# Block inversion of 8 triangular 128x128 matrices: full tiles against 64x64 quadrants

## The reference

```
x = silu(causal_conv(hidden @ w_qkvz));  q, k, v, z = split(x)
beta = sigmoid(b);  g = -exp(A_log) * softplus(a + dt_bias)
for t in positions:                       # per value head
    state = state * exp(g_t)
    delta = (v_t - state.T k_t) * beta_t
    state = state + outer(k_t, delta)
    o_t   = state.T q_t
y = rmsnorm(o * silu(z)) @ w_out
```

## Time and profile before

| what | value |
|---|---|
| three runs | 3936.69 us median, 3885.03 to 3954.14 |
| span of the profiled execution | 3551.5 us, the only time that its page gives |
| busy: PE, PE loads, DVE, ACT, POOL | 3065.3, 2458.8, 3248.5, 1811.4, 1861.5 us |
| mean granted clock of TensorE | 0.935 of full speed |
| DMA | 435.09 MB, mean 123 GB/s |

### The profile page before, as it was taken

One profiled execution on the slowest core, in us unless ns is written; L12 is line 12 of the kernel. 1 busy time (PEld: TensorE's weight loads), 2 busy tenths in 40 slices (PEclk: granted clock), 3 DMA queues, 4 the chain that ended last, 5 costly groups with the idle time before them and its releaser, 6 DMA issues.

```text
span 3551.5 us, 58967 instructions
## 1 busy us (share of the span) xinstructions
PE 3065.3 (86%) x18512; PEld 2458.8 (69%) x18512; DVE 3248.5 (91%) x10343; ACT 1811.4 (51%) x4134; POOL 1861.5 (52%) x1973
## 2 busy tenths in 40 slices
PE   6761799989998899989999898989999899989997
PEld 3330577767777677767777777777777677777776
DVE  7888899989999899989999899989998899989997
ACT  2231455545555455555555555555555555555554
POOL 0001565556665566545665555655556555565555
PEclk8885799999999999999999999999999999999999
DMA  1000555545554455444554454445454454544554
GB/s 58 1 1 25 135 139 137 136 121 147 133 136 129 123 144 133 129 121 134 147 133 132 132 135 133 131 119 141 131 143 127 125 141 130 143 127 137 135 141 136
DMA packets 550338, 435.09 MB, mean 123 GB/s; under 512 B 250976, under 2 KB 457824, under 8 KB 549984
## 3 DMA queue, kind: packets, MB, share of 16 engines
q1 hardware_dynamic: 483424, 226.34, 23.9%
q0 software_dynamic: 66560, 204.54, 20.9%
HBM read 350.93 MB, written 45.74 MB: 112 GB/s over the span
## 4 chain that ended last, share of the span: by engine, by line
DVE 58%; PE 27%; issue 8%; POOL 3%; DMA 3%; DVEq 1%; SPq 1%; ACT 0%; POOLq 0%; ACTq 0%
DVE qkv L1082 12%; PE ps L523 6%; DVE rows L1098 6%; PE ps L510 6%; PE ps L530 6%; DVE mix L1110 5%; DVE outer L1119 5%; DVE xr L1123 5%; PE ps L476 4%; DVE xg L1052 3%; DVE E L1070 2%; DVE acc L1047 2%; POOL rows L857 2%; PE ps L493 2%; DVE acc L1183 2%
## 5 line engine op out<-in xcount | busy, mean ns | idle before, releaser
L857 POOL DMA_INDIRECT rows<-table,pick x1040 | 1047.2, 1007 | 363.9 <-issue 335.7
L715 ACT ACTIVATE qkv<-qkv 128x512 f32<-128x512 f32 x260 | 163.8, 630 | 710.8 <-DVE qkv L1082 710.8
L1082 DVE SCALAR_TENSOR_TENSOR qkv<-raw,cwv,qkv 128x510 f32<-128x510 f32 (+2 forms) x390 | 467.5, 1199 | 6.9
L530 PE MATMUL ps<-XT,E 128*128 128x128 f32 x3072 | 412.2, 282 | 0.0
L510 PEld LDWEIGHTS ps<-X,AT 128*128 128x128 f32 x3072 | 375.4, 197 | 51.0 <-issue 42.3
L523 PEld LDWEIGHTS ps<-E,XT 128*128 128x128 f32 x2048 | 270.0, 202 | 165.1 <-DVE E L1070 132.4
L530 PEld LDWEIGHTS ps<-XT,E 128*128 128x128 f32 x3072 | 381.5, 198 | 0.0
L510 PE MATMUL ps<-X,AT 128*128 128x128 f32 x3072 | 381.2, 278 | 0.3 <-DMA XT<-whole 0.3
L1110 DVE SCALAR_TENSOR_TENSOR mix<-rows,zc,mix 128x256 f32<-128x256 f32 x896 | 374.9, 475 | 0.0
L523 PE MATMUL ps<-E,XT 128*128 128x128 f32 x2048 | 293.2, 289 | 83.6 <-DVE E L1070 83.6
L710 ACT ACTIVATE raw<-ps 128x512 f32<-128x512 f32 x260 | 155.2, 597 | 342.8 <-PE ps L476 342.4
(11 more groups left out here) (167 smaller groups left out, 6844.2 us busy)
## 6 DMA issues: line engine op xcount, KB each, us to landing
Wvz<-wvz SPq DMA_DIRECT2D x65, 512.0 KB, 3.2
xb<-xnT SPq DMA_DIRECT2D x65, 512.0 KB, 4.3
whole<-AT SPq DMA_DIRECT2D x130, 256.0 KB
X<-whole SPq DMA_DIRECT2D x130, 256.0 KB, 3.3
XT<-whole SPq DMA_DIRECT2D x130, 256.0 KB, 4.0
Wkq<-wkq SPq DMA_DIRECT2D x66, 256.0 KB, 3.6
rows<-table,pick POOLq DMA_INDIRECT x1040
wo<-woh SPq DMA_DIRECT2D x65, 256.0 KB, 4.0
```

The source lines that it names most:

```text
L530: done = mm(ps[:, 4 + g, (a % 4) * P:(a % 4 + 1) * P], E[:, a, :], src[:, a, :], start=True, stop=True)
L857: pool.indirect_dma_start(rows[:, m, :], None, table[:, :], bass.IndirectOffsetOnAxis(ap=pick[:, m:m + 1], axis=0)).then_inc(gathered, 16)
L1082: ins = V.scalar_tensor_tensor(out=o, in0=i, scalar=w, in1=o, op0=ALU.mult, op1=ALU.add)
```

## The change

The levels of 16 and 32 are done on the two diagonal 64x64 quadrants alone, with a tile of 64 columns for each of 8 tasks, so that a result for all tasks fits one bank. A matmul takes rows 0 to 63 or 64 to 127 of its operands and writes the same partitions. Of E only the columns of the first block of each pair come out of matmuls (32 of 64, `firsts`); the others are the identity, copied once into E16 and E32 at the start. The last level becomes one 64x64 corner: minus (A's corner times X64 of the lower half) is copied by ACT with scale -1, and XT of the upper half times it gives the corner of XT. XT's other corner is set to zero once. The lower quadrant alone is needed in X64. Y gets a buffer of its own. X16 and XT16 are read as quadrants, by four DMAs as before, of half the bytes. Waits follow: PE now waits for ACT's `e_s` where it waited for DVE's fifth `e_v`, and the wait on `acc_v` for bank 3 and that on `qs_s` stand later on PE; POOL waits for the whole of level 32 (`e_v` 2).

```
+    H = P // 2;  lower, upper = slice(0, H), slice(H, P);  halves = (lower, upper)
+        def firsts(ap, n):
+            return ap.rearrange("p a (b s c) -> p a b s c", s=2, c=n)[:, :, :, 0, :]
-                    sp.wait_ge(sm["xt_t"], at("xt_t", 2))
-                for g in range(2):
-                    for s, dst in enumerate((X16, XT16)):
-                        sp.dma_start(dst[:, 4 * g:4 * g + 4, :], matrices(1 + s, g)).then_inc(sm["inv_in"], 16)
+                    sp.wait_ge(sm["xt_t"], at("xt_t", 1))
+                for s, dst in enumerate((X16, XT16)):
+                    for h in halves:
+                        sp.dma_start(dst[h, :, :], matrices(1 + s)[h, :, h]).then_inc(sm["inv_in"], 16)
...
                 def level_E(lv):
-                    src = X16 if lv == 0 else X
-                    for g in range(2):
-                        if lv:
-                            pe.wait_ge(sm["x_s"], at("x_s", 2 * (lv - 1) + g + 1))
-                        for a in range(4 * g, 4 * g + 4):
-                            done = mm(ps[:, g, (a % 4) * P:(a % 4 + 1) * P], AT_b[:, a, :], src[:, a, :], start=True, stop=True)
-                        done.then_inc(sm["e_t"], 1)
+                    src, n = ((X16, 16), (X32, 32))[lv]
+                    if lv:
+                        pe.wait_ge(sm["x_s"], at("x_s", lv))
+                    for a in range(TASKS):
+                        for h in halves:
+                            done = mm(ps[h, 0, a * 32:a * 32 + 32], AT_b[h, a, h], firsts(src[h, a:a + 1, :], n),
+                                      start=True, stop=True)
+                    done.then_inc(sm["e_t"], 1)
...
+                def level_X(lv):
+                    src, E = ((XT16, E16), (XT32, E32))[lv]
+                    if lv:
+                        pe.wait_ge(sm["xt_s"], at("xt_s", lv))
+                    pe.wait_ge(sm["e_v"], at("e_v", lv + 1))
...
+                    for a in range(TASKS):
+                        for h in halves[:2 - lv]:
+                            done = mm(ps[h, 2, a * H:(a + 1) * H], src[h, a, :], E[h, a, :], start=True, stop=True)
+                    done.then_inc(sm["x_t"], 1)
...
+                    for a in range(TASKS):
+                        for h in halves:
+                            done = mm(ps[h, 4, a * H:(a + 1) * H], E[h, a, :], src[h, a, :], start=True, stop=True)
+                    done.then_inc(sm["xt_t"], 1)
+                def corner_E():
+                    pe.wait_ge(sm["x_s"], at("x_s", 2))
+                    for a in range(TASKS):
+                        done = mm(ps[upper, 0, a * H:(a + 1) * H], AT_b[lower, a, upper], X64[lower, a, :], start=True, stop=True)
+                    done.then_inc(sm["e_t"], 1)
+                def corner_XT():
+                    pe.wait_ge(sm["xt_s"], at("xt_s", 3))
+                    pe.wait_ge(sm["e_s"], at("e_s", 1))
+                    for a in range(TASKS):
+                        done = mm(ps[lower, 4, a * H:(a + 1) * H], E64[upper, a, :], XT[upper, a, upper], start=True, stop=True)
                     done.then_inc(sm["xt_t"], 1)
...
-                    level_X(1, 0)
-                    level_X(1, 1)
-                    level_E(2)
+                    level_X(1)
+                    corner_E()
+                    if place["u"]:
+                        pe.wait_ge(sm["acc_v"], last("acc_v", 2))
...
-                    pe.wait_ge(sm["e_v"], at("e_v", 5))
+                    pe.wait_ge(sm["e_s"], at("e_s", 1))
...
+                def compact(dst, bank, h=slice(0, P), scale=1.0):
+                    return A(dst, ps[h, bank, :].rearrange("p (a i) -> p a i", a=TASKS), ACT.Copy, scale=scale)
+                def take_X(lv):
+                    act.wait_ge(sm["x_t"], at("x_t", lv + 1))
+                    if lv == 0:
+                        compact(X32[:, :, :], 2).then_inc(sm["x_s"], 1)
+                    else:
+                        compact(X64[lower, :, :], 2, lower).then_inc(sm["x_s"], 1)
+                def take_XT(lv):
...
+                    elif lv == 1:
+                        for h in halves:
+                            compact(XT[h, :, h], 4, h).then_inc(sm["xt_s"], 1)
+                    else:
+                        compact(XT[lower, :, upper], 4, lower).then_inc(sm["xt_s"], 1)
+                def take_corner():
+                    act.wait_ge(sm["e_t"], at("e_t", 3))
+                    compact(E64[upper, :, :], 0, upper, -1.0).then_inc(sm["e_s"], 1)
...
-                def level(lv, g):
-                    dve.wait_ge(sm["e_t"], at("e_t", 2 * lv + g + 1))
-                    V.tensor_tensor(E[:, 4 * g:4 * g + 4, :], ps[:, g, :].rearrange("p (a i) -> p a i", a=4), mask(C_MS + lv, 4), ALU.mult)\
-                        .then_inc(sm["e_v"], 1)
+                def level(lv):
+                    E, n = ((E16, 16), (E32, 32))[lv]
+                    dve.wait_ge(sm["e_t"], at("e_t", lv + 1))
+                    m = cst[:, T_MS + 32 * lv:T_MS + 32 * lv + 32].rearrange("p (b c) -> p b c", c=n)
+                    V.tensor_tensor(firsts(E[:, :, :], n), ps[:, 0, 0:256].rearrange("p (a b c) -> p a b c", a=TASKS, c=n),
+                                    m.unsqueeze(1).broadcast_to([P, TASKS, 32 // n, n]), ALU.mult).then_inc(sm["e_v"], 1)
...
-                    level(2, 0)
-                    level(2, 1)
                     expert_mix(4, 6)
```

More of the change, by code:

```diff
@@ L69, in level @@
     def level(n):
-        off = (p // (2 * n) == j // (2 * n)) & (p // n == j // n + 1)
-        return np.eye(P) - off
+        q, c = p % H, np.array([c for c in range(H) if c // n % 2 == 0])[None, :]
+        off = (q // (2 * n) == c // (2 * n)) & (q // n == c // n + 1)
+        return (q == c) - 1.0 * off
     eye = np.broadcast_to(np.eye(BL).reshape(1, BL * BL), (P, BL * BL))
-    m = [np.eye(P), p <= j, p > j, p < j, eye[:, :P], eye[:, P:]] + [level(n) for n in LEVELS]
+    m = [np.eye(P), p <= j, p > j, p < j, eye[:, :P], eye[:, P:]]
     m = np.stack([np.asarray(a, np.float32) for a in m], 1).reshape(P, NC * P)
@@ L361, in _ @@
             clear(GROUPS)
[L362 to L364 removed]
+            sp.wait_ge(zeroed, 1)
+            for s in range(2):
+                sp.dma_start(matrices(1 + s), XT[:, :, :]).then_inc(loaded, 16)
             sp.wait_ge(loaded, LOADS + 32)
@@ L611, in one_pass @@
                     pe.wait_ge(sm["S_s"], at("S_s", 1))
+                    if place["u"]:
+                        pe.wait_ge(sm["qs_s"], last("qs_s"))
                     for w, bank in ((KCH, 1), (QCH, 5)):
@@ L757, in one_pass @@
                 if back:
-                    for g in range(2):
-                        take_X(1, g)
-                        take_XT(1, g)
+                    take_X(1)
+                    take_XT(1)
+                    take_corner()
                 silu(1)
```

101 lines of the change are left out of this document (43 added, 58 removed).

## The result

The changed kernel took 4173.36 us in the median of 4 runs (4170.59 to 4181.92), the kernel before 3944.86 in 4 runs on the same chip (3885.03 to 3954.14): a ratio of 1.0645, with a 95% interval of 1.0597 to 1.0694. It is slower by 229 us, where I forecast 38 less.

A forecast was written before the change was run, and what follows sets the result against it. Neither PE nor DVE alone was taken to bound the kernel; the chain alternates between them. Earlier steps summed to 0.6 us a pass, 64 x 0.6 = 38 us off 3936.69, about 3900 us; range 3785 to 4000.

The forecast's parts named there:

- what lies around the span (385 us): Runs' median lies 385 us above the profiled span of 3551.5; taken as outside it and unchanged by the edit.
- the corner's new wait: Last level: PE waits for ACT's copy of the corner product; costed at nothing, 0.6 us without cover.
- The record's price: PE's 64-column records: 0.056 us each, between 0.028 and 0.111; 208 cost 11.6 us a pass, for 14.2 before.
- Rival 1: PE's levels: two quadrants run side by side, 0.04 us or less a record; some 100 us gained, 3840; chance 0.29.
- the mask on the first products: DVE's mask after the levels of 16 and 32: claimed to come only 0.27 us earlier in a pass.
- the 200 us forecast: DVE's level operations: six of 0.66 us become two of 0.41, removing 3.1 us a pass, 200 us in all.
- DVE's busy time falling by less than some 200 us: Sign that the forecast is wrong: DVE's busy time over the run doesn't fall by some 200 us.
- the two acc sums: DVE's sums into acc beside POOL's xg products: first slips out short, second is held long.
- Borders between tile sizes: PE entering or leaving small tiles, eight a pass: 0.2 us each, between 0 and 0.27, covered by gaps or slack.
- The elimination: DVE's elimination after the acc sums: claimed to get going about 0.5 to 0.7 us earlier in a pass.
- Rival 2: PE between first E and products: records don't halve; gain gone at 62 ns, 4350 us at 0.111; chance 0.15.
- Rival 3: PE's granted clock falls to 1.2 GHz in the level stretches: 100 to 200 us lost, 4040 to 4140; chance 0.06.

The follow-up runs named there:

- e5: Changed kernel, no edit, run on chip 14: 3515.89 us, 0.9818 of the kernel before.
- e10: Changed kernel, no edit, run on chip 0: 3510.08 us, 0.9803 of the kernel before.
- e17: Changed kernel with the transposed X of the level of 32 computed three times, 64 more records a pass, on chip 11: 4043.43 us in one run.
- E64: Not a run: the last level's corner product, minus A's corner times X of the lower half, copied by ACT with scale -1; no time of its own.
- e16: Changed kernel without the gathers of expert rows, on chip 11: 3392.4 us in one run.
- e3: Changed kernel without the gathers of expert rows, on chip 13: 3405.91 us, 0.9493 of the kernel before.
- e15: Changed kernel with the lower quadrant for all tasks first, then the upper, in both levels, on chip 11: 4137.22 us in two runs.
- e18: Changed kernel with two pairs of expert mixes moved ahead of the masks on the products, on chip 11: 4159.9 us, 1.0705 of the kernel before.
- e12: Changed kernel with two pairs of expert mixes moved ahead of the masks on the products, on chip 0: 3483.5 us, 0.9733 of the kernel before.
- e2: Changed kernel with the lower quadrant for all tasks first, then the upper, in both levels, on chip 13: 3733.21 us, 1.0406 of the kernel before.
- e8: Changed kernel with 24 unread filler matmuls a pass added where PE waits: 3592.53 us, 1.0045 of the kernel before.

## Why the prediction was wrong

**The step that failed** is "I take what lies around the span (385 us) as unchanged". The prediction moved a sum made on one chip to a median from another. The profiled execution of before is one of a chip on which this kernel takes 3580; the timed runs came from one on which it takes 3945. On chips of the first sort (e5, e10) the change gives 0.98 of before, the direction that the working gave: 63 and 66 us, where it said 38. On the second sort 4 us a pass are lost. What I took as unchanged, the distance between the two kinds of chip, is 366 us in the kernel before (3944.86 - 3579.04) and 657 in the changed one (4173.36 - 3515.89): it grew by 291.7 us, and that less the gain of 63.2 is the measured loss of 228.5. One sign was there to read: a span far below the lowest timed run (3885) says that the two may not be the same population. The result brought the other: every run has about 2 us around its span, none anything near 385. The very execution whose trace I summed is among e5's runs of before, 3553.28 us on chip 14; e5's profiled run is 37 us shorter. That this meets the forecast 38 is luck: the records, the borders, the first mask and the sums into acc each came out otherwise, as told below, and 3553.28 is among the fastest of 19 runs whose median is 3579.04.

**What the slow kind adds.** Passes, as the mean distance of two zc (L1133, L1179): before 49.07 us in the first profile, 54.74 on chip 11; the changed kernel 48.57 on chip 14, 58.89 in its first profile. So the chip costs before 5.7 us a pass and the changed kernel 10.3. (54.74 and 58.89 are from two chips that agree on before within 1%, 3912 and 3945; no run timed both kernels on chip 11.) Where it comes in, as medians over 63 passes, each time from the pass's zc (fast is the first profile):

```
                                 before, fast / chip 11     changed, chip 14 / first chip
mask on the first products          10.1 / 10.7                8.5 /  9.5
mask on the second products, kq     20.4 / 25.7               18.6 / 26.1
gated outputs                       30.8 / 35.9               29.6 / 42.2
expert dots of the next pass        43.9 / 49.5               42.7 / 54.2
```

Up to kq before loses 4.7 us beyond what it lost at the first mask, the changed kernel 6.5; from there to the gated outputs (L1052, L1096) before loses nothing more, the changed kernel another 5.1. The late increments come 11.4 to 11.9 us in the median behind the first gather of their half (in all traces and halves but the first of e17), 1 to 2 us after the last of its eight issues has ended: PE's results are held until POOL's gathers are through.

*Up to kq.* In the kernel before fewer of a pass's steps behind them wait for each other: its third E is DVE's, and kq at 1955.06 follows without a wait. In the changed kernel everything behind XT stands in series on PE's word: ACT's two copies of XT (idle 528.9 us, 356.3 of them ended by the unknown queue), E64 (the view's "ACT E L758"), then

```profile
L613 PE MATMUL ps<-cst,qkv 128*128 128x128 f32 x128 | 43.8, 445 | 215.7 <-ACT E L758 208.2 <-issue 7.2
```

a wait of which before has nothing near that size. I had costed the corner's new wait at nothing, with the price "if the cover is gone" 0.6 us; it is 3.3 us of PE's time a pass here, and nothing on chips 14 and 0. But this chain ends at kq, and from the first mask to kq the changed kernel loses only 1.8 us more than before (6.5 against 4.7). No run took the corner's wait away, so that this chain makes the 1.8 is argued and not shown. That gathers are a necessary part is shown (e16 and e3).

*Behind kq.* The larger part, 5.1 us (of which some comes back later in the pass, 4.6 are left of all), arises where no instruction of the changed levels stands but the corner's XT (L562): from kq to the gated outputs. There DVE waits for the first application in every pass, in the kernel before on chip 11 in 40 passes for 113.2 us in all:

```profile
L1096 DVE SCALAR_TENSOR_TENSOR xg<-ps,rq,z 128x256 f32<-128x256 f32 x128 | 56.1, 480 | 260.7 <-remote 260.7
```

And there PE runs at the lower of its two clocks. The granted clock over the 8 us from kq on is 0.56 in the changed kernel's first profile, after PE's long waits; 0.91 in the kernel before on chip 11, 0.99 in e5. The same two groups, first profile and e5:

```profile
2070.88 1.96 PE L562 MATMUL ps<-XT,E 64*64 64x64 f32 x16
2072.77 3.53 PE L493 MATMUL ps<-xnT,Wvz 128*128 x4
...
1866.91 1.14 PE L562 MATMUL ps<-XT,E 64*64 64x64 f32 x16
1867.99 1.98 PE L493 MATMUL ps<-xnT,Wvz 128*128 x4
```

Those are 2.4 us that lie between kq and the application. The passes can be sorted by that clock; from kq to the first gated output, medians in us, number of passes in brackets:

```
                                   clock under 0.95     0.95 and over
changed, first chip                  16.13 (60)          11.16 (3)
e15, in turn, chip 11                16.11 (54)          11.59 (9)
e17, XT three times, chip 11         16.11 (7)           11.16 (56)
e18, mixes moved, chip 11            15.36 (57)          11.97 (6)
before, chip 11                      12.38 (25)          10.94 (38)
```

In a pass with PE at full clock this stretch takes nearly what it takes in e5 (10.71), though the trace is of the slow kind and the gathers run beside it. Where the clock is low, the output comes in the four versions of the changed kernel at 11.5 to 11.6 us behind the second gathers' first issue, which is when what was held is let go; where it is high mostly at 7.3. I read it so: the slow clock makes the application 2 to 3 us late, its results then fall under the hold, and that makes 5 of it. The sorting is by what happened to the passes and not by an edit, so this too is argued and not shown. But it accounts for e17, whose PE records wait longer in the first half and whose clock is back by kq (0.95).

**The record's price,** taken as 0.056 between 0.028 and 0.111: 0.027 to 0.032 as the quadrants alternate (32 records of L541 in 1.15 us: (1.15 - 0.22)/31 = 0.030), 0.052 in turn. The steps that have one quadrant alone (X of level 32 and both corners, 48 of the 208 records) stand 0.0615 apart at full clock in e5 and 0.110 at half in the first profile's L562. So 160 records at 0.027 to 0.032 and 48 at 0.0615 make 7.3 to 8.1 us a pass, for 11.6 forecast. Rival 1 was right on the size for what alternates. Its sign came too: DVE waits for the E of level 32 no more (2.1 us before L1116 in the whole of e5), and the mask on the first products is 1.65 us early for the 0.27 of the forecast. It reached its 100 us only in part: of Rival 1's 1.3 to 1.8 us a pass, 1.0 came, and DVE's dots took back what the next paragraph says.

**DVE.** L1116 takes 53.3 us for 128, 0.416 each, against 0.41 taken; the levels fell from 253.3 to 53.3, the 200 us forecast. The prediction named DVE's busy time falling by less than some 200 us as a sign that it is wrong, and so it came: DVE's busy time between the first profile and e5 fell only from 3248.5 to 3101.7, by 147. The dots (L1098 257.1 to L1144 312.7) took 56 back. Each is 0.28 us, but 1.11 when POOL's product `gm` (L886) runs beside it (the two at 1844.44 and 1845.48 in e5's timeline, under POOL's 2.22 us from 1844.23). In e5 all 106 dots of over 0.9 us overlap a two-input operation of POOL, and none of the 835 that don't overlap one is over 0.9.

It is the effect that I had placed on the two acc sums. Those went from 1.13 in the median for the first to a median of 0.425 for both (means of 0.54 and 0.71): most slip out, where I had one short and one long, and the loss moved to the dots. In e12 the dots are back to 260.2 and the time is 27 us less; that the one makes the other wasn't tried by itself, as the mixes also fill DVE's waits for PE.

**Borders between tile sizes,** taken at 0.2 where they aren't covered: none is visible (L554 at 1862.38 to L608 at 1863.34: 15 records in 0.96 us, 0.064 each, border included, for 0.0615 inside such a group). The drain that the Trainium skill (TensorEngine Tiling, Key Properties) names at a change of tiling mode costs nothing that these rows show.

**The elimination** was to start 0.5 to 0.7 us earlier; on chip 14 it starts at 23.40 after zc against 25.15, 1.7 earlier, since kq is 1.9 earlier (1.2 forecast). The gated outputs are still 1.2 earlier, and the dots of the next pass 1.2.

**Rival 2** (records that don't halve) didn't happen; its end, slower by over 2%, did, on the slow kind, by a cause that was on no list. **Rival 3** was right in direction: the clock fell from 0.93 to 0.90 to 0.91 on fast chips and to 0.842 in e2. But e12 is faster at 0.868 than e10 at 0.90, and e8 slower at 0.912: on these chips the mean clock doesn't decide. At the first chip it is 0.809, and its half-speed stretches come after PE's waits (the second products, L510, took 2.05 us at 2067.40 against 1.13 at 2052.82, both on 8 matmuls), on the path to the gated outputs. There Rival 3, given 0.06, may describe the larger part of what the changed kernel loses beyond before, though by another road: PE had waited.

**What stays open.** Whether the slow kind is the chip's own: each chip was timed in a few minutes only, so something else that ran on it then would look the same, and before's two runs at 4090 us between others at 3911 say that more than the chip's number counts. What holds PE's increments beside gathers. The transfers don't look it: a gather's packets take 175 ns in the median on both kinds, and the packets that bring instructions 0.98 us in the first profile of after against 1.01 in e5. Whether it is the semaphore's way, PE's own issue (the fours every 0.75 us, and 11% "issue" in e17's chain) or the recording itself wasn't tried apart: every run here comes with its span and clock. Whether the changed kernel would lose 5 us less a pass there if PE's clock stayed up behind kq: e8's fillers weren't run on such a chip. And why e17's clock is back sooner.

## What to carry to other kernels

Before a sum is made on a profile, see that its span plus what lies around it (here 1.8 to 2 us) is one of the timed runs. If it isn't, profile and times may be of different chips, and the sum needs a second case, for the chip whose times count. A chain that hands over between engines at every step has more to lose where handing over is slow, and an engine that waits may come back at the lower clock: read the clock of the stretch behind a long wait, not the run's mean. Both are how I read these traces; no run isolates them. Matmuls in quadrants pay in full only if neighbours in the queue go to different quadrants, and DVE's dots and sums stretched up to fourfold here beside long two-input operations of POOL, so a saving on DVE can be given back by the work that slides there (e5, e12).

## What the runs showed of the hardware

- Chips differ by up to 10% on the same kernel: 3575.81 to 3586.36 in the medians of chips 13, 14 and 0, 3565.76 and 3574.69 on chip 1, and 3862.61 to 3911.69 in four runs on chip 11, with two more at 4090. The difference comes with PE's semaphore increments late beside indirect gathers (730 of 2822 against 0; 2.7 us in the median there, 3.4 in the changed kernel) and is gone without gathers (3392.4, changed kernel). Whether it is the chip or what ran on it then wasn't tried.
- On such a chip a long run of PE's small matmuls is itself held beside gathers: 207.7 us of PE's idle time before L547 in e17, none in e5.
- 64x64 fp32 records: 0.027 to 0.032 us apart alternating between two quadrants, 0.052 in one quadrant after the other, 0.0615 where a step has one quadrant alone; all at full clock.
- DVE's 128x128 dot product takes 0.28 us and up to 1.18 beside POOL's two-input operations (e5: 106 of 189 over 0.9 beside them, 0 of 835 otherwise).
- The granted clock went down with the smaller records (0.93 to 0.90) and further with the quadrants in turn (0.842), with PE busy 80% and more; 24 added matmuls a pass raised it by 0.006 only.
